# Last stage: VectorE takes the scores out of PSUM with the maxima added, in place of a matmul that picked them

## The reference

```python
var = jnp.mean(jnp.square(hidden_states), axis=-1, keepdims=True)
normed = hidden_states * jax.lax.rsqrt(var + EPS) * norm_w
q = split_heads(normed @ wq)              # (8, 16, 512, 64)
k = split_heads(key_value_states @ wk)
v = split_heads(key_value_states @ wv)
scores = jnp.einsum('bhqd,bhkd->bhqk', q, k)
attn = jax.nn.softmax(scores, axis=-1)
ctx = jnp.einsum('bhqk,bhkd->bhqd', attn, v)
return hidden_states + merge_heads(ctx) @ wo
```

## Time and profile before

| | |
|---|---|
| median of 3 runs | 5056.27 us (5054.94 to 5061.84) |
| the profiled execution's own time | 5050.86 us |
| its span, first to last instruction | 5049.1 us |
| busy over the span | PE 92%, DVE 60%, ACT 46%, POOL 19% |
| last stage | about 3835 us to 5049 us |
| 4432 to 4576 us, eight pairs of the last stage | of 144 us: PE 142.36, DVE 72.08, ACT 53.32, POOL 53.16 |

### The profile page before, as it was taken

One profiled execution on the slowest core, in us unless ns is written; L12 is line 12 of the kernel. 1 busy time (PEld: TensorE's weight loads), 2 busy tenths in 40 slices (PEclk: granted clock), 3 DMA queues, 4 the chain that ended last, 5 costly groups with the idle time before them and its releaser, 6 DMA issues.

```text
span 5049.1 us, 66199 instructions
## 1 busy us (share of the span) xinstructions
PE 4650.1 (92%) x24484; PEld 1878.1 (37%) x24484; DVE 3031.1 (60%) x7970; ACT 2308.9 (46%) x3011; POOL 968.6 (19%) x831
## 2 busy tenths in 40 slices
PE   6899999889998999999899988899889999999999
PEld 2333333333333333343444433333333333333333
DVE  5777776556777777666466675455534455545554
ACT  3455554456664444434455554444443333333332
POOL 0111111101110111111111111111113343333333
PEclk9999999999999999999999999999999999999999
DMA  1111111121121110001211211111120000000000
GB/s 57 37 44 58 48 41 44 35 78 64 58 65 52 35 39 32 31 30 44 70 63 59 68 62 49 37 37 34 39 76 21 10 3 13 13 13 13 1 13 9
DMA packets 152306, 201.55 MB, mean 40 GB/s; under 512 B 18993, under 2 KB 102321, under 8 KB 150706
## 3 DMA queue, kind: packets, MB, share of 16 engines
q1 hardware_dynamic: 151986, 197.31, 11.7%
HBM read 128.86 MB, written 68.42 MB: 39 GB/s over the span
## 4 chain that ended last, share of the span: by engine, by line
PE 59%; issue 18%; DVE 15%; ACT 4%; DMA 3%; POOL 1%; SPq 0%; DVEq 0%; POOLq 0%; ACTq 0%
PE psO L720 8%; PE small L649 7%; PE small L656 6%; PE psT L695 5%; PE psT L925 5%; PE psS L677 4%; DVE nmb L1169 4%; PE psT L778 3%; PE psT L649 2%; PE psT L885 2%; PE psO L940 2%; PE psT L895 2%; PE psT L940 2%; DVE nmb L1166 2%; DVE xn L1146 2%
## 5 line engine op out<-in xcount | busy, mean ns | idle before, releaser
L989 ACT ACTIVATE probs<-psT 128x1024 f32<-128x1024 f32 (+3 forms) x1280 | 1160.3, 961 | 1262.3 <-PE psT L695 1091.0
L1169 DVE TENSOR_REDUCE nmb<-psS 128x1 bf16<-128x512 f32 x1024 | 649.2, 685 | 279.2 <-PE psS L677 279.1
L1166 DVE CUSTOM_DVE_ANT_0 out<-psS,pens_sb 128x512 f32<-128x512 f32 x1024 | 665.7, 686 | 242.3 <-issue 241.1
L695 PE MATMUL psT<-low 32*128 32x512 f32 (+3 forms) x5120 | 750.0, 604 | 27.9 <-ACT probs L989 24.5
L677 PE MATMUL psS<-out 32*128 32x512 bf16 (+3 forms) x2560 | 592.6, 376 | 104.2 <-DVE nmb L1166 49.9
L720 PE MATMUL psO<-probs,V 128*32 128x512 f32 (+3 forms) x5120 | 658.1, 586 | 28.2 <-DVE probs L1178 26.6
L1352 DVE TENSOR_REDUCE parts<-psS 128x2 bf16<-128x1024 f32 x256 | 315.0, 1230 | 531.1 <-PE psS L912 531.1
L1095 ACT ACTIVATE probs<-psT 128x1024 f32<-128x1024 f32 x256 | 262.2, 1024 | 524.8 <-PE psT L928 524.8
L677 PEld LDWEIGHTS psS<-out 32*128 32x128 bf16 x2560 | 148.5, 91 | 800.8 <-issue 439.2
L778 PE MATMUL psT<-out,W 128*128 128x512 f32 x768 | 382.8, 620 | 0.4
L1019 ACT ACTIVATE low<-small,vec 128x256 f32<-128x256 f32 (+1 forms) x464 | 262.3, 618 | 231.7 <-PE small L649 231.7
(11 more groups left out here) (177 smaller groups left out, 5659.1 us busy)
## 6 DMA issues: line engine op xcount, KB each, us to landing
o_mid<-out SPq DMA_DIRECT2D x160, 256.0 KB, 2.0
oN<-o_mid SPq DMA_DIRECT2D x160, 128.0 KB
oN<-r_mid SPq DMA_DIRECT2D x80, 256.0 KB
x_mid<-xe SPq DMA_DIRECT2D x40, 512.0 KB, 2.9
xw<-x_mid SPq DMA_DIRECT2D x36, 512.0 KB, 4.1
xe<-x_mid SPq DMA_DIRECT2D x36, 512.0 KB, 5.0
cT<-ctxT SPq DMA_DIRECT2D x20, 512.0 KB, 7.5
W<-wm SPq DMA_DIRECT2D x6, 1024.0 KB, 7.8
```

The source lines that it names most:

```text
L695: last = nc.tensor.matmul(psT[j][:, q0:S], Kf[rows_of(j), q, a, c, kt * P:(kt + 1) * P], Qf[rows_of(j), q, a, c, q0:S], start=True, stop=p ...
L989: nc.scalar.activation(probs[:, i % 2, two, q0:S], psT_all[:, two, q0:S], ACT.Exp, scale=float(DH) ** -0.5)\
L1166: nc.vector.tensor_tensor_reduce(junk[:, e, 0:n], psS[e][:, 0:n], penalty, 1.0, -3.0e38, ALU.add, ALU.max, at).then_inc(sem[f"s_read{e}"], 1)
L1169: nc.vector.tensor_reduce(at, psS[e][:, 0:n], AX, ALU.max).then_inc(sem[f"s_read{e}"], 1)
```

## The change

1. VectorE takes the scores of a block out of the two banks, adds the negated maxima, and writes them to `probs` (`tail_lower`, new). ScalarE's exponential then runs in place on `probs`. The two picking matmuls go. The scores of block at + 1 now wait for `tail_lowered`, VectorE's count, and no longer for the exponential.
2. The maxima come as two fills for each pair (one for each head), whose weights repeat one column 128 times, so that every row of the bank holds the maxima. ScalarE reads both out into `m5`.
3. These two fills stand in block 2 ahead of `s`, where one stood in block 3.
4. The bf16 scores run six blocks ahead (`AHEAD5`), where they ran five.
5. Of the k projection ScalarE writes the bf16 copy first. `tail_set` and the memsets of `pick_max` go.
6. At the start the first unit's x leads the queue behind the constants, then `Wqkv`, ctx and the masks; `Wo`, `W1` and `W2` follow.

```diff
 def tail_extras(n, kt):
+    if kt == 2 and n + 1 < PAIRS:
+        names += [f"m{n + 1}_{j}" for j in range(2)]
     if kt == 2 and n:
         names.append(f"s{n - 1}")
-    if kt == 3 and n + 1 < PAIRS:
-        names.append(f"m{n + 1}")
...
+AHEAD5 = T + 2
...
                     sp.dma_start(xw[:], src).then_inc(sem["x_in"], 16)
+                    if cur is None:
+                        sp.dma_start(Wqkv[:], wa[0, :, 0:N_QKV]).then_inc(qkv_in, 16)
...
                 elif kind == "m":
                     for qt in range(T):
-                        last = nc.tensor.matmul(dst[:, qt * P:(qt + 1) * P], nmb[i % 2][:, qt, :], identb[:], start=True, stop=True)
+                        maxima = nmb[i % 2][:, qt, DL * part:DL * part + 1]
+                        maxima = bass.AP(tensor=maxima.tensor, offset=maxima.offset, ap=[list(maxima.ap[0]), [0, P]])
+                        last = nc.tensor.matmul(dst[:, qt * P:(qt + 1) * P], maxima, identb[:], start=True, stop=True)
...
             def tail_exp_scores(at):
                 n, kt = divmod(at, T)
-                if kt == 0:
-                    name = f"m{n}"
-                    pe.wait_ge(tail_small_read[tail_bank(name)], tail_fills(name) + 2)
-
                 if at:
-                    pe.wait_ge(tail_exp_done, at)
+                    pe.wait_ge(tail_lowered, at)
                 for j in range(2):
                     rows = slice(DL * j, DL * (j + 1))
-                    nc.tensor.matmul(psT[j], K5[n % 3][rows, kt * P:(kt + 1) * P], Q5[n % 3][rows, :], start=True, stop=False)
-                for j in range(2):
-                    rows = slice(DL * j, DL * (j + 1))
-                    last = nc.tensor.matmul(psT[j], pick_max[rows, :], mrows[n % 2][rows, :], start=False, stop=True)
+                    last = nc.tensor.matmul(psT[j], K5[n % 3][rows, kt * P:(kt + 1) * P], Q5[n % 3][rows, :], start=True, stop=True)
                 last.then_inc(tail_st_full, 1)
...
             def tail_exponentials(at):
-                n, kt = divmod(at, T)
-                act.wait_ge(tail_st_full, at + 1)
-
-                if n:
-                    act.wait_ge(tail_pv_done, at - T + 1)
-                    act.wait_ge(tail_summed, 3 * (n - 1) + max(kt, 1))
-                nc.scalar.activation(P5[kt], psT_all[:, 0:2, :], ACT.Exp).then_inc(tail_exp_done, 1)
+                act.wait_ge(tail_lowered, at + 1)
+                nc.scalar.activation(P5[at % T], P5[at % T], ACT.Exp).then_inc(tail_exp_done, 1)
...
+            def tail_lower(at):
+
+                n, kt = divmod(at, T)
+                if kt == 0:
+                    for j in range(2):
+                        name = f"m{n}_{j}"
+                        dve.wait_ge(tail_small_read[tail_bank(name)], tail_fills(name) + 2)
+                dve.wait_ge(tail_st_full, at + 1)
+
+                if n:
+                    dve.wait_ge(tail_pv_done, at - T + 1)
+                    dve.wait_ge(tail_summed, 3 * (n - 1) + max(kt, 1))
+                nc.vector.tensor_tensor(P5[kt], psT_all[:, 0:2, :], m5[:, n % 2], ALU.add).then_inc(tail_lowered, 1)
...
             for at in range(T * PAIRS):
                 n, kt = divmod(at, T)
                 b, m = divmod(n, NP)
-                if at + T + 1 < T * PAIRS:
-                    tail_maximum(at + T + 1)
+                tail_lower(at)
+                if at + AHEAD5 < T * PAIRS:
+                    tail_maximum(at + AHEAD5)
```

More of the change, by code:

```diff
@@ L174, in tail_extras @@
     return names
-TAIL_FIRST = [f"x0_{c}" for c in range(C)] + ["q0", "k0", "q1", "k1"] + [f"v0_{i}" for i in range(2 * T)] + ["m0"]
-TAIL_MIXED = len(TAIL_FIRST) - 1
+TAIL_FIRST = [f"x0_{c}" for c in range(C)] + ["q0", "k0", "q1", "k1"] + [f"v0_{i}" for i in range(2 * T)] + [f"m0_{j}" for j in range(2)]
+TAIL_MIXED = len(TAIL_FIRST) - 2
+AHEAD5 = T + 2
 TAIL_EARLY = TAIL_MIXED - 3
@@ L327, in build @@
         tail_exp_done = semaphore("tail_exp_done")
+        tail_lowered = semaphore("tail_lowered")
         tail_pv_done = semaphore("tail_pv_done")
@@ L398, in build @@
         scratch = sb("scratch", [P, 16])
-        parts = sb("parts", [P, 8 * S + P], BF16)
+        parts = sb("parts", [P, 8 * S], BF16)
         low5 = sb("low5", [P, 2, 8 * S])
@@ L457, in build @@
         kb5 = [parts[:, i * S:(i + 1) * S] for i in range(2, 4)]
-        mrows = [parts[:, i * S:(i + 1) * S] for i in range(4, 6)]
+        m5 = gel_flat[:, 4 * S:8 * S].rearrange("p (i j n) -> p i j n", i=2, j=2)
         nmb_flat = parts[:, 6 * S:8 * S]
         nmb = [nmb_flat[:, i * S:(i + 1) * S].rearrange("p (t n) -> p t n", t=T) for i in range(2)]
-        pick_max = parts[:, 8 * S:8 * S + P]
         x5 = [xw, xe]
@@ L595, in _ @@
                 sp.dma_start(dst, src).then_inc(consts_in, 16)
[L596 to L599, removed]
             for n, _ in enumerate(walk(sp, body)):
                 s, kind = divmod(n - 1, 3)
+                if n == 0:
+                    sp.dma_start(Wo[:], wa[0, :, N_QKV:]).then_inc(wo_in, 16)
+                    sp.dma_start(W1[:], wm1[0]).then_inc(wm_in, 16)
+                    sp.dma_start(W2[:], wm2[0]).then_inc(wm_in, 16)
                 if n >= 1 and s < 5 and kind == 0:
@@ L804, in mlp @@
                     maximum_next(m)
-                    if cur is None and m >= FC - T - 1:
-                        tail_max_scores(m - (FC - T - 1))
+                    if cur is None and m >= FC - AHEAD5:
+                        tail_max_scores(m - (FC - AHEAD5))
                 if cur is not None:
@@ L945, in _ @@
             pe.wait_ge(consts_set, 3)
-            pe.wait_ge(wm_in, 32)
             for n, _ in enumerate(walk(pe, body)):
                 s, kind = divmod(n - 1, 3)
+                if n == 1:
+                    pe.wait_ge(wm_in, 32)
                 if n >= 1 and s in (1, 3) and kind == 2:
@@ L955, in _ @@
             pe.wait_ge(small_read, FILLS + 1)
-            pe.wait_ge(tail_set, 2)
-            tail_fill(TAIL_FIRST[-1])
+            for name in TAIL_FIRST[TAIL_MIXED:]:
+                tail_fill(name)
             for i in range(2 * T):
@@ L963, in _ @@
                 tail_exp_scores(at)
-                if at + T + 1 < T * PAIRS:
-                    tail_max_scores(at + T + 1)
+                if at + AHEAD5 < T * PAIRS:
+                    tail_max_scores(at + AHEAD5)
                 for name in tail_extras(n, kt):
@@ L1079, in tail_take @@
                 elif kind == "k":
-                    nc.scalar.activation(K5[i % 3], src[:], ACT.Copy)
-                    last = nc.scalar.activation(kb5[i % 2], src[:], ACT.Copy)
+                    nc.scalar.activation(kb5[i % 2], src[:], ACT.Copy)
+                    last = nc.scalar.activation(K5[i % 3], src[:], ACT.Copy)
                 elif kind == "v":
@@ L1084, in tail_take @@
                 else:
-                    last = nc.scalar.activation(mrows[i % 2], src[:], ACT.Copy)
+                    last = nc.scalar.activation(m5[:, i % 2, part, :], src[:], ACT.Copy)
                 last.then_inc(tail_small_read[bank], 1)
             def tail_exponentials(at):
-                n, kt = divmod(at, T)
-                act.wait_ge(tail_st_full, at + 1)
-                if n:
-                    act.wait_ge(tail_pv_done, at - T + 1)
-                    act.wait_ge(tail_summed, 3 * (n - 1) + max(kt, 1))
-                nc.scalar.activation(P5[kt], psT_all[:, 0:2, :], ACT.Exp).then_inc(tail_exp_done, 1)
+                act.wait_ge(tail_lowered, at + 1)
+                nc.scalar.activation(P5[at % T], P5[at % T], ACT.Exp).then_inc(tail_exp_done, 1)
             act.wait_ge(consts_in, 16 * 4)
@@ L1107, in _ @@
                     limits(Unit(2, 0, 0)).then_inc(pensS, 1)
-            tail_take(TAIL_FIRST[-1])
+            for name in TAIL_FIRST[TAIL_MIXED:]:
+                tail_take(name)
             for at in range(T * PAIRS):
@@ L1292, in mlp @@
                         maximum(nxt, n // 2, n % 2)
-                    if cur is None and n <= T:
+                    if cur is None and n < AHEAD5:
                         tail_maximum(n)
@@ L1385, in _ @@
                     nc.vector.memset(nmb_flat, 0.0)
[L1386 to L1390, removed]
                     tail_moments_of(0)
```

3 lines of the change are left out of this document (1 added, 2 removed).

## The result

The changed kernel takes 5238.38 us (median of 4 runs, 5234.87 to 5247.33) against 5059.06 us (4 runs, 5054.94 to 5067.8) for the kernel before on the same chip: 1.0353 times as long, 95% interval 1.0338 to 1.0369. That is 179 us slower, where 5223 was forecast and 5175 to 5265 given as the range.

A forecast was written before the change was run, and what follows sets the result against it. TensorE's stream was taken to bound the last stage. Terms -41.7 - 16.7 + 158.7 + 35.6 + 3 - 7 gave +132, clock +35, total +167 on 5050.86 profiled: 5218, plus 5.4 for the median: 5223 us, range 5175 to 5265.

The forecast's parts named there:

- The wait for the bank: Block 2 of 62 pairs: `s` waits for ScalarE's read-out of the first maxima, starting 2.56 us later; +158.7 us.
- The reciprocal ahead of the next step: 20 pairs without v or y fills: reciprocal delays VectorE's block 3 step, so next scores wait 2.26 us; net +35.6 us.
- The picking matmuls: Removing them saves a TensorE slot of 0.215 us, counted in 194 of 256 blocks; -41.7 us.
- rival 4: Waits are not on the path as ScalarE and VectorE answer in time; -60 us, 4996 us; 2%.
- The clock: Holes of about 2.2 us in 62 pairs halve TensorE's clock 25 times, 1.4 us each; +35 us.
- Four in ten: Assumed share of the 62 holes that bring a clock fall, taken between none and all.
- The last pair: Reciprocal also stands ahead of its block 3 step, with no later work to cover it; about +3 us.
- The start: Weights no longer load before the masks, so the compute chain behind all moves earlier; -7 us.
- The clock that stays up: Waits as forecast, but TensorE's clock never falls; 5188 us; 18%.
- the fall at every hole: Each of 62 holes costs the clock, 105 us in place of 35; 5293 us; 5%.
- The slower step: VectorE's step takes over 1.24 us beside GpSimd's sums; at 1.38, 11 us more, 5234 us; over 1.38: 3%.
- The faster one: Waits are not on the path, needing `s` to start at 1.8 instead of 4.05; 4996 us; 2%.

The follow-up runs named there:

- The halves: Kernel after, in the 20 pairs without v or y fills only the reciprocal's first half ahead of block 3's step, second half and scaling behind step and maximum: 5209.18 us.
- the halves with the filled hole: Kernel after with the reciprocal split around block 3's step, and the second maxima fill's matmuls issued nine times over in block 2: 5177.99 us.
- both waits shortened: Kernel after with the maxima read out ahead of block 2's exponential, and the reciprocal split around block 3's step: 5070.89 us.
- the experiment on the start alone: Kernel before with only Wo, W1 and W2 moved behind the masks, last stage unchanged: 5058.34 us, ratio 0.9993.

## Why the prediction was right

The forecast was right in sign, mechanism and place; the sum was 15 us short of the median. Against the profiled spans the sum was 5049.1 + 167 = 5216, measured 5238.6, so 22 us more; the median lies 0.2 us under the span, and the forecast had put it 7 over, which takes back 7. Step by step:

**The wait for the bank**: `s` at 4.05 forecast, 4.12 measured, in every one of 62 pairs: 2.63 us each, 163 us where 158.7 was forecast. In its parts, from start to start: scores to VectorE's step 1.17 (forecast 1.18), to the exponential 1.26 (1.30), to the first read-out 0.97 (0.92), to `s` 0.72 (0.65). VectorE's step is 1223 ns, taken as 1.24 us. The exponential is 1056 ns from SBUF, where from PSUM it was 1.02: some 0.03 us a pair. By the Trainium skill, "VectorE: DVE Perf Modes", section "The TRN2 errata", the estimate was 0.04 us, from ScalarE's larger fixed cost with an SBUF source; the trace agrees. Reading the maxima out first removed most of this, which shows the cause.

**The reciprocal ahead of the next step**: 2.16 us of hole for 2.26 forecast. Per pair, over what the other pairs pay, it is 3.42 - 1.80 + 0.09 = 1.71 for 1.78 forecast (19.09 - 15.67 = 3.42 for a pair behind one of its kind; 0.09 for the different saving on the fill of maxima). The halves gave back 1.6. The step holds. In the pairs with v or y fills it cost nothing, as forecast: these are 1.80 (v) and 1.79 (y) longer without a fall, 1.88 with x fills in the kernels where these have none, and the terms of the prediction that bear on them, 2.56 - 3 x 0.215 - 0.24, give 1.68.

**The picking matmuls**: their slot of 0.215 us is exact where TensorE is never waited for. Over the kernel before as a whole it is 45 us rather than 55. Inside the forecast nothing was wrong with it, since in the 20 pairs the waits of VectorE had been counted by themselves. In rival 4, which saves the whole 55 and the waits too, it was counted too well.

**The clock**: 25 falls and 35 us forecast, 29 falls in pairs 1 to 62 and an estimated 38 us measured (1.64 to 1.66 us a fall where TensorE is the bound, 0.4 to 0.9 in most plain pairs, where a fall lies partly in the second wait). "Four in ten" was a middle value between none and all, and the right one was 29 in 62, so the count was luck. The price of a fall was reasoned, as half of 3.4 us less what lies in a wait, and held: 1.7 for 1.65 where TensorE is the bound, 1.4 for 38 / 29 = 1.3 in the mean. The experiments show the cause: with the second hole closed the falls go from 31 to 18, and with the first one filled too to 3, while `s` starts as late as before. They show as well that the number wasn't to be had by counting holes: filling the first moved falls to the second. The Trainium skill, "TensorE: Matmul & The Clock Gate", section "HAM oscillation", tells of a loop whose waits of some 3 to 5 us for transfers cost the clock in every round. The holes here are shorter and come back as regularly, and the trace agrees only in part: 29 of 62 pairs lost it.

**The last pair**: +4.6 us (37.7 to 42.3) where 3, less 0.9 for its four slots, was forecast; the clock falls there too. Pair 0 gained 0.6.

**The start**: 6.3 us where 7 was forecast, but "it all moves" failed: the last stage began 2.3 us later, 8.6 us off that step, the largest part of what the sum lacked. The profiled executions of the eight kernels with the new queue, whose five stages ahead differ by next to nothing, begin it between 3837.7 and 3850.5 us (3838.2 for the halves with the filled hole, 3850.5 for both waits shortened); the two with the old queue begin it at 3835.4 and 3851.9 us. A gain of 6 us is smaller than that scatter. Whether it is lost in the loops or only hidden by them stays open: the experiment on the start alone ended some 3.5 us lower by its ratio, with an interval that holds both.

Added up against the profiled span, in us: waits and slots in the pairs +7, clock +3.5, last pair +2.5, start +9, together the 22.

**The rivals.** The clock that stays up (5188) and the fall at every hole (5293) are both refuted by the 29 of 62. The slower step (5234) is refuted by its 1223 ns, though its time lay nearest to the measured one: by chance, as the terms above show. The faster one needed `s` at 1.8 and got 4.12.

## What to carry to other kernels

When a result is put into a bank taken in turn, ask who reads out what stood there, and what that reader has in front of it in its own queue: here two read-outs behind one exponential made a chain of four steps on three engines, and moving them ahead of it gave back 126 us. A wait can also be kept and covered, by issuing work that nobody waits for between the fill and the next claim on its bank (the outputs, another 20 us). And price a matmul taken away by who would be waited for next in each kind of iteration: in two thirds of the pairs it was TensorE's whole slot, in the others half.

## What the runs showed of the hardware

A hole of 2.2 us in TensorE's work was followed by 3.41 us at 1.2 GHz in 29 of 62 pairs, at the same places of nearly every sequence, and the price was 1.64 to 1.66 us of a pair where TensorE was the bound. Three of these falls began in the second hole, which has 2.16 us and comes 20 times; with the first hole filled, 19 of the 20 second holes brought one. In the two kernels whose regular holes were only of 0.44 or 0.56 us in each pair the clock fell in the last two pairs alone. Filling the wait with matmuls whose result is already there is a way to see, in a kernel, what the clock alone costs.

VectorE's sum over 1024 columns with one operand in PSUM and one in SBUF takes 1223 ns in the mean of 256, as much as the maximum over 1024 columns of PSUM (1.23 us). GpSimd's sums, which read the same memory, make no difference: it is 1224 ns in the 107 that run beside one for 30% of their time or more, and 1222 in the others.
